# One scan of 1024 columns over two channel tiles in place of two scans of 512, with both exponentials in one double PSUM tile

## The chip, the cores and the metric

The kernel runs on one core of a Trainium2 chip. The metric is the device time of one execution in microseconds (us). Everything is float32.

## What is computed

A decoder layer over 16 sequences of 128 tokens and 1024 features: a selective scan (Mamba) block, a cross attention, a routed low-rank feed-forward, each followed by a layer norm. The change touches the first alone. Its core:

```python
proj = hidden_states @ W_in.T
x, gate = (proj[..., :D_IN], proj[..., D_IN:])
...
x = jax.nn.silu(xc)                      # xc: causal convolution of x over time
...
dt = jax.nn.softplus(ts @ W_dt.T + b_dt)
A = -jnp.exp(A_log.astype(jnp.float32))
def step(state, inp):
    dt_t, B_t, C_t, u_t = inp
    dA = jnp.exp(dt_t[..., None] * A)
    state = state * dA + (dt_t * u_t)[..., None] * B_t[:, None, :]
    y = jnp.einsum('bdn,bn->bd', state, C_t)
    return (state, y)
...
y = ys.transpose(1, 0, 2) + x * D
y = y * jax.nn.silu(gate)
return y @ W_out.T
```

D_IN is 2048 channels, N is 16 states for each channel.

## The kernel before

The scan stage cuts the work into 4 groups g of 4 sequences (GT = 512 columns, one for each token of the group) and 4 quads q of QD = 4 channel tiles of 128 channels. A pair (g, q) is a step, s = 4g + q, 16 in all. Each step has 16 turns, one for each state n. What happens for one n is spread over four engines:

- GpSimd (line 1144) multiplies dtu (dt times u) by the row of B and writes hb[n % 4], 128 x 2048: all four channel tiles at once.
- ScalarE (act_step, line 522) computes exp(dt * A) for each channel tile i = 0 to 3 into a PSUM bank, bank(i % 2). Column 0 of each sequence in banks 0 and 1 is zero throughout (they are cleared once), and the exponential writes the other 127, so that a scan over several sequences starts anew at each.
- VectorE (dve_scan, line 662) scans tile i in place: h[t] = exp[t] * h[t-1] + h[t], over 512 columns.
- TensorE (turn, line 306) transposes the scanned tiles, four blocks into bank 2 or 3 for one sequence b; VectorE (dve_acc, line 678) multiplies this by C and adds it to acc.

The order on each engine is that of the program text; semaphores join the engines. VectorE scans two states ahead: while it accumulates state n it scans n + 2. A turn has two halves. In each, VectorE does two accumulations (b = 2 part, 2 part + 1), and then two scans (i = 2 part, 2 part + 1). After the second half of turns n = 8 to 15 follows one output addition (dve_out, line 687), in n = 10 and 12 two additions for dt of the next step (dve_dt, line 652), in n = 1 and 3 of q = 1 the layer norm's statistics and application. Between steps VectorE does the skip connection and the gate (lines 745, 754).

ScalarE does, beside the exponentials: a copy of a gate tile after those of n = 3, 5, 7 and 9 (line 530), Silu of the gates after those of n = 10, with a load of its table before it and of the exponential's behind it (lines 533, 534), and for the next step the softplus of two channel tiles each after those of n = 11 and n = 13 (lines 507 to 511: Abs, Exp, Ln). Since ScalarE is two states ahead too, these stand where VectorE is in the turns n = 8, 9 and 11. The last step (s = 15) prepares no next one.

Semaphores: an exponential waits for scan_ok, so that the scan two tiles earlier is over (e - 1 + SCAN with SCAN = 2, the count that scan_ok has at the outset); a scan waits for exp_ok of its own tile, and the first of a state for bm_ok of GpSimd. TensorE waits for all scans of its state (line 330). The eight PSUM banks lie in four tensors banks[0] to banks[3] of two banks each; bank(i) is half of one.

Of the kernel before, what the change touches and what calls it, by code (L numbers as in the profile page):

```python
# [19 lines left out]
ALU = mybir.AluOpType  # L20
# [9 lines left out]
D_IN, N, R = 2048, 16, 64  # L30
# [3 lines left out]
GT = GB * SEQ  # L34
NG = TOK // GT
QD = 4
# [15 lines left out]


X_MM, CONV, SS_ADD = 8, 8, 4
T_DONE, SCAN, ACCD, R_ADD, FIN1, FIN, Z_MM, BM = 13, 2, 2, 2, 2, 5, 2, 13
ONE = 1

SEMS = """const_loaded xt_loaded0 xt_loaded1 xt_loaded2 xt_loaded3 pool_const rows_set bdt_loaded a_exp a_neg x_mm conv_base conv_tap conv_done u_done
# [12 lines left out]
def program(nc, a, out):  # L71
# [5 lines left out]
    with ExitStack() as ctx:  # L77
# [3 lines left out]
        S = {name: ctx.enter_context(nc.semaphore(name)) for name in SEMS}  # L81
# [23 lines left out]
        hb = [at(8192 + 2048 * i, QD * GT) for i in range(4)]  # L105
# [74 lines left out]
        def bank(i):  # L180
            return banks[i // 2][:, (i % 2) * HALF:(i % 2 + 1) * HALF]

        def following(g, q):
            return (g, q + 1) if q < NQ - 1 else (g + 1, 0)
# [110 lines left out]
        def pe_step(pe, g, q, last=False):  # L295
            s = NQ * g + q
            if q == 0:
                pe.wait_ge(S["xg_loaded"], 16 * g + 16)
            for n in range(N):
                U = N * s + n  # L300

                def turn(b):

                    pe.wait_ge(S["acc_ok"], 4 * U + b - 1 + ACCD)
                    for i in range(QD):
                        last = nc.tensor.transpose(bank(2 + b % 2)[:, i * P:(i + 1) * P],  # L306
                                                   hb[n % 4][:, i * GT + b * P:i * GT + (b + 1) * P],
                                                   ident[:, :])
                    last.then_inc(S["t_done"], 1)

                def filler(part):
                    if n < 8:
                        i = n // 2
                        if n % 2 == 0 and part == 0:
                            pe.wait_ge(S[f"wz_loaded{i % 2}"], 16 * (2 * s + i // 2 + 1))
                            if i < 2:
                                pe.wait_ge(S["r_added"], 8 * s + i - 1 + R_ADD)
                            else:
                                pe.wait_ge(S["z_copied"], 4 * s + i - 1)
                        for k in range(4 * (n % 2) + 2 * part, 4 * (n % 2) + 2 * part + 2):  # L320
                            last = nc.tensor.matmul(bank(6 + i % 2), wz[i % 2][:, k, :], xg[:, k, :],  # L321
                                                    start=(k == 0), stop=(k == KC - 1))
                        if k == KC - 1:
                            last.then_inc(S["z_mm"], 1)
                    else:
                        if n == 8 and part == 0:
                            pe.wait_ge(S["wo_loaded"], 16 * s + 16)
                        pe_out(pe, s, n - 8, range(2 * part, 2 * part + 2))

                pe.wait_ge(S["scan_ok"], 4 * U + 4 + SCAN)  # L330
                turn(0)
                turn(1)
                filler(0)
                turn(2)
                turn(3)
                filler(1)
                if not last and n in (7, 11):
                    for i in ((0, 1) if n == 7 else (2, 3)):
                        if i >= 2:
                            pe.wait_ge(S["dt_ok"], 4 * (s + 1) + i - 1)  # L340
                        else:
                            pe.wait_ge(S["fin1"], 4 * s + i - 1 + FIN1)
                        pe_dt(pe, *following(g, q), i)

            pe.wait_ge(S["acc_ok"], 4 * (N * s + N) + ACCD)
            for i in range(QD):
                if i < 2 and not last:
                    pe.wait_ge(S["dt_ok"], 4 * (s + 1) + 3 + i)
                else:
                    pe.wait_ge(S["fin1"], 4 * s + i - 1 + FIN1)  # L350
                for b in range(GB):
                    last = nc.tensor.transpose(bank(4 + i % 2)[:, b * P:(b + 1) * P],
                                               acc[:, b, i * P:(i + 1) * P], ident[:, :])
                last.then_inc(S["yt_mm"], 1)
# [158 lines left out]
        def act_step(act, g, q, last=False):  # L513
            s = NQ * g + q
            for n in range(N):
                for i in range(QD):
                    e = 4 * (N * s + n) + i
                    if n == 0:
                        act.wait_ge(S["dt_ok"], 4 * s + i + 1)

                    act.wait_ge(S["scan_ok"], e - 1 + SCAN)
                    nc.scalar.activation(by_seq(bank(i % 2))[:, :, 1:SEQ],  # L522
                                         by_seq(dt[q % 2][:, i, :])[:, :, 1:SEQ], ACT.Exp,
                                         scale=a_sb[:, QD * q + i, n:n + 1]).then_inc(S["exp_ok"], 1)
                if n in (3, 5, 7, 9):
                    i = (n - 3) // 2
                    if i == 0:
                        act.wait_ge(S["fin"], 4 * s + FIN)
                    act.wait_ge(S["z_mm"], 4 * s + i + 1 + Z_MM)
                    nc.scalar.activation(zs[:, i, :], bank(6 + i % 2), ACT.Copy).then_inc(S["z_copied"], 1)  # L530
                if n == 10:
                    act.wait_ge(S["z_copied"], 4 * s + 4)
                    nc.scalar.activation(zs, zs, ACT.Silu).then_inc(S["z_silu"], 1)
                    act.preload_act_table_set(LN_EXP_SET)
                if not last and n in (11, 13):
                    act_softplus(act, *following(g, q), (0, 1) if n == 11 else (2, 3))
# [115 lines left out]
                nc.vector.scalar_tensor_tensor(d, bank(4 + i % 2), 0.0, d, ALU.max, ALU.add)\  # L652
                    .then_inc(S["dt_ok"], 1)

        def dve_scan(dve, g, q, n, i):

            U = N * (NQ * g + q) + n
            if i == 0:
                dve.wait_ge(S["bm_ok"], U + 1 + BM)
            dve.wait_ge(S["exp_ok"], 4 * U + i + 1)  # L660
            h = hb[n % 4][:, i * GT:(i + 1) * GT]
            nc.vector.tensor_tensor_scan(h, bank(i % 2), h, 0.0, ALU.mult, ALU.add)\  # L662
                .then_inc(S["scan_ok"], 1)

        def dve_acc(dve, g, q, n, b):
# [50 lines left out]
        def dve_step(dve, g, q, last):  # L716
            s = NQ * g + q
            for n in range(N):

                if n < N - 2:  # L720
                    scans = [(g, q, n + 2, i) for i in range(QD)]
                else:
                    scans = [] if last else [(*following(g, q), n + 2 - N, i) for i in range(QD)]
                if q == 1 and n == 8:
                    dve.wait_ge(S["r_loaded"], 16 * g + 16)
                for part in range(2):
                    dve_acc(dve, g, q, n, 2 * part)
                    dve_acc(dve, g, q, n, 2 * part + 1)
                    for unit in scans[2 * part:2 * part + 2]:
                        dve_scan(dve, *unit)  # L730
                if n >= 8:
                    dve_out(dve, s, n - 8)
                if not last and n in (10, 12):
                    dve_dt(dve, *following(g, q), (0, 1) if n == 10 else (2, 3))
                if q == 1 and n == 1:
                    dve_ln_stats(dve, g)
                if q == 1 and n == 3:
                    dve_ln_apply(dve, g)

            dve.wait_ge(S["o_mm"], 8 * s + 8 + ONE)  # L740
            dve.wait_ge(S["z_silu"], s + 1)

            def skip(i):
                dve.wait_ge(S["yt_mm"], 4 * s + i + 1 + ONE)
                nc.vector.scalar_tensor_tensor(yq[:, i, :], uq[q % 2][:, i, :],  # L745
                                               dsk[:, QD * q + i:QD * q + i + 1], bank(4 + i % 2),
                                               ALU.mult, ALU.add).then_inc(S["fin1"], 1)

            skip(0)
            for i in range(QD):  # L750
                if i < QD - 1:
                    skip(i + 1)
                dve.wait_ge(S["fin1"], 4 * s + i + 1 + FIN1)
                nc.vector.tensor_tensor(yq[:, i, :], yq[:, i, :], zs[:, i, :], ALU.mult)\
                    .then_inc(S["fin"], 1)
# [404 lines left out]
        def _(dve):  # L1160
# [73 lines left out]
            dve.wait_ge(S["phase0_c"], 1)  # L1234
            dve.wait_ge(S["phase0_zero"], 2)
            dve_dt(dve, 0, 0, range(QD))
            for i in range(2 * QD):
                dve_scan(dve, 0, 0, i // QD, i % QD)

            with nc.vector.Fori(0, NG - 1) as g:  # L1240
                dve_group(dve, g, last=False)
# [80 lines left out]
```

## Time and profile before

| | us |
|---|---|
| median of 3 timed runs | 3447.59 |
| lowest, highest | 3445.62, 3452.21 |
| span of the profiled execution, first to last instruction | 3444.0 |
| busy in the span: TensorE (matmul) | 2894.4 |
| busy: VectorE | 2815.9 |
| busy: ScalarE | 1403.2 |
| busy: GpSimd | 1399.2 |
| VectorE's 1024 scans among it | 1189.3 |

The span is the profiled execution's own time between its first and its last instruction; the timed runs, which are other executions, also hold what lies around it. PE is TensorE's matmul, PEld its weight load, DVE is VectorE, ACT ScalarE, POOL GpSimd. A busy share is an average over stages: the projection and convolution come first (to about 550 us), then the scan stage (to about 2680 us), then attention and feed-forward.

### The profile page before, as it was taken

What the parts mean: (1) busy time and instruction counts of PE and PEld (TensorE: products, weight loads), DVE (VectorE), ACT (ScalarE), POOL (GpSimd) and SP (SyncE); (2) the same over time, 40 slices, a digit from 0 to 9 for tenths busy, and PEclk for the clock granted to TensorE, in tenths of its full rate; (3) what the DMA queues carried; (4) which work ended last, traced back from release to release, by engine and by line L of the source; (5) the groups of instructions that cost most, each with busy time, mean ns of one, the idle gap of its engine ahead of it and who ended that gap; (6) DMA issues with size and microseconds to landing.
All of it is one profiled execution on the core that took longest, in us unless ns stands there. A gap on an engine that the chain in (4) does not pass through costs nothing.

```text
span 3444.0 us, 37416 instructions
## 1 busy us (share of the span) xinstructions
PE 2894.4 (84%) x10992; PEld 1521.9 (44%) x10992; DVE 2815.9 (82%) x3919; ACT 1403.2 (41%) x2166; POOL 1399.2 (41%) x455
## 2 busy tenths in 40 slices
PE   7999996877887877887877887877877999999996
PEld 3445453444443434444434444434443455555553
DVE  2333336999999999999999999999998677777775
ACT  1111113534434534534534534534532455555553
POOL 0000004555565565565555665555662122222221
PEclk9999997999999999999999999999999999999998
DMA  4111114120113120113120113120112121111110
GB/s 145 55 55 38 54 49 116 57 110 7 56 62 80 55 104 7 62 50 87 62 100 11 62 50 86 61 89 22 61 37 62 42 75 61 61 61 55 55 61 25
DMA packets 57906, 210.48 MB, mean 61 GB/s; under 512 B 4481, under 2 KB 4609, under 8 KB 52961
## 3 DMA queue, kind: packets, MB, share of 16 engines
q1 hardware_dynamic: 57762, 208.76, 18.2%
q8 instruction: 66, 1.08, 0.1%
q14 instruction: 78, 0.64, 0.1%
HBM read 172.96 MB, written 35.78 MB: 61 GB/s over the span
## 4 chain that ended last, share of the span: by engine, by line
PE 35%; DVE 34%; issue 20%; POOL 4%; ACT 4%; DVEq 2%; DMA 1%; SPq 0%; POOLq 0%; ACTq 0%
DVE arena L662 16%; PE banks L1004 13%; DVE arena L678 10%; PE banks L407 3%; PE banks L450 3%; PE banks L363 2%; PE banks L388 2%; POOL arena L1138 2%; POOL arena L1144 2%; PE banks L418 2%; DVE rbuf L687 2%; PE banks L289 1%; PE banks L378 1%; PE banks L986 1%; DVE arena L745 1%
## 5 line engine op out<-in xcount | busy, mean ns | idle before, releaser
L1144 POOL TENSOR_TENSOR arena<-arena 128x2048 f32<-128x2048 f32 x256 | 1156.9, 4528 | 620.4 <-PE banks L306 618.2
L662 DVE TENSOR_TENSOR_SCAN arena<-banks,arena 128x512 f32<-128x512 f32 x1024 | 1189.3, 1201 | 36.2 <-POOL arena L1144 19.8
L522 ACT ACTIVATE banks<-arena,a_sb 128x508 f32<-128x508 f32 x1024 | 700.1, 687 | 1151.6 <-DVE arena L662 1151.4
L306 PE MATMUL banks<-ident,arena 128*128 128x128 f32 x4096 | 665.2, 292 | 385.5 <-DVE arena L678 350.4
L306 PEld LDWEIGHTS banks<-ident,arena 128*128 128x128 f32 x4096 | 460.7, 146 | 871.7 <-DVE arena L678 712.8
L678 DVE SCALAR_TENSOR_TENSOR arena<-banks,cg,arena 128x512 f32<-128x512 f32 x960 | 664.1, 731 | 1.3 <-PE banks L306 1.0
L289 PE MATMUL banks<-arena 128*128 128x512 f32 x1088 | 523.6, 606 | 5.4 <-issue 5.4
L321 PE MATMUL banks<-arena 128*128 128x512 f32 x1024 | 501.4, 614 | 0.0
L1004 PE MATMUL banks<-arena 128*128 128x512 f32 x1024 | 444.5, 595 | 24.6 <-DMA dsk<-in_D 24.6
L1197 DVE SCALAR_TENSOR_TENSOR arena<-banks,arena 128x508 f32<-128x508 f32 (+2 forms) x192 | 142.6, 742 | 330.8 <-ACT arena L1070 326.3
L1138 POOL TENSOR_TENSOR arena<-arena 128x2048 f32<-128x2048 f32 x16 | 72.4, 4526 | 711.8 <-DMA arena<-u_scratch 551.5
L633 POOL TENSOR_TENSOR arena<-arena,qr 128x512 f32<-128x512 f32 x128 | 141.2, 1103 | 474.0 <-DVE qr L800 474.0
L1004 PEld LDWEIGHTS banks<-arena 128*128 128x128 f32 x1024 | 194.2, 191 | 262.8 <-issue 262.8
L289 PEld LDWEIGHTS banks<-arena 128*128 128x128 f32 x1088 | 192.2, 196 | 149.3 <-issue 149.3
L321 PEld LDWEIGHTS banks<-arena 128*128 128x128 f32 x1024 | 182.3, 199 | 129.3 <-issue 129.3
L785 DVE TENSOR_REDUCE qm<-banks 128x8 f32<-128x512 f32 x128 | 88.1, 688 | 100.2 <-PE banks L407 100.2
L1070 ACT ACTIVATE arena<-banks,arena 128x512 f32<-128x512 f32 x64 | 49.8, 778 | 264.0 <-PE banks L1004 264.0
L559 ACT ACTIVATE arena<-arena 128x512 f32<-128x512 f32 x128 | 80.7, 631 | 159.7 <-DVE arena L789 159.2
L407 PE MATMUL banks<-arena 128*128 128x512 f32 x256 | 133.9, 605 | 0.9 <-issue 0.9
L388 PE MATMUL banks<-arena 128*128 128x512 f32 x256 | 121.2, 596 | 0.0
L363 PE MATMUL banks<-arena 128*128 128x512 f32 x256 | 120.5, 593 | 0.0
L450 PE MATMUL banks<-arena 128*128 128x512 f32 x256 | 115.1, 593 | 0.7 <-issue 0.7
(131 smaller groups left out, 2481.0 us busy)
## 6 DMA issues: line engine op xcount, KB each, us to landing
arena<-in_WoutT SPq DMA_DIRECT2D x17, 2048.0 KB, 8.0
arena<-in_WinZ SPq DMA_DIRECT2D x64, 512.0 KB, 3.4
arena<-in_xT SPq DMA_DIRECT2D x8, 2048.0 KB, 15.3
u_scratch<-arena SPq DMA_DIRECT2D x16, 1024.0 KB, 5.9
arena<-b_scratch SPq DMA_DIRECT2D x16, 1024.0 KB, 19.9
arena<-u_scratch SPq DMA_DIRECT2D x16, 1024.0 KB, 10.0
arena<-x_scratch SPq DMA_DIRECT2D x32, 512.0 KB, 3.5
x_scratch<-rbuf SPq DMA_DIRECT2D x5, 2048.0 KB, 7.5
```

Source lines behind the costliest of these rows:

```text
L289: last = nc.tensor.matmul(bank(6 + c % 2), yq[:, k, (c // 2) * P:(c // 2 + 1) * P], wo[:, k, (c % 2) * HALF:(c % 2 + 1) * HALF], start=(k ...
L306: last = nc.tensor.transpose(bank(2 + b % 2)[:, i * P:(i + 1) * P], hb[n % 4][:, i * GT + b * P:i * GT + (b + 1) * P], ident[:, :])
L321: last = nc.tensor.matmul(bank(6 + i % 2), wz[i % 2][:, k, :], xg[:, k, :], start=(k == 0), stop=(k == KC - 1))
L363: last = nc.tensor.matmul(bank(2 + h), wk[:, o * P:(o + 1) * P], cn[:, h * HALF:(h + 1) * HALF], start=True, stop=True)
L388: last = nc.tensor.matmul(bank(6), cT[:, t, :], ekT[:, t, :], start=(t == 0), stop=(t == NT - 1))
L407: nc.tensor.matmul(bank(t % 2), x1[:, t * P:(t + 1) * P], wq, start=True, stop=True)\
L450: last = nc.tensor.matmul(bank(5 + 2 * h), mt[:, o, :], qs[:, o, h * HALF:(h + 1) * HALF], start=(o == 0), stop=(o == OT - 1))
L522: nc.scalar.activation(by_seq(bank(i % 2))[:, :, 1:SEQ], by_seq(dt[q % 2][:, i, :])[:, :, 1:SEQ], ACT.Exp, scale=a_sb[:, QD * q + i, n:n + ...
L662: nc.vector.tensor_tensor_scan(h, bank(i % 2), h, 0.0, ALU.mult, ALU.add)\
L678: last = nc.vector.scalar_tensor_tensor(acc[:, b, :], bank(2 + b % 2), c, acc[:, b, :], ALU.mult, ALU.add)
L1004: last = nc.tensor.matmul(bank(tg), wx[par][:, k, :], xT[:, k, tg * GT:(tg + 1) * GT], start=(k == 0), stop=(k == KC - 1))
L1144: nc.gpsimd.tensor_tensor(hb[n % 4].rearrange("p (i t) -> p i t", i=QD), dtu, brep[:, n:n + 1, :].broadcast_to([P, QD, GT]), ALU.mult)\
```

## The change

The two exponentials of a half (i = 0 and 1, or 2 and 3) go to the two banks of banks[0] as before, and one scan of 1024 columns reads both at once. The column of zeros at each sequence's start separates the second channel tile from the first as it separates sequences. scan_ok now counts halves instead of tiles: the first exponential of a half waits until the scan of the half before has ended (SCAN = 1), the second has no wait of its own; the scan waits for both exponentials. The order of the accumulations, additions and scans on VectorE stays.

```diff
-T_DONE, SCAN, ACCD, R_ADD, FIN1, FIN, Z_MM, BM = 13, 2, 2, 2, 2, 5, 2, 13
+T_DONE, SCAN, ACCD, R_ADD, FIN1, FIN, Z_MM, BM = 13, 1, 2, 2, 2, 5, 2, 13
...
-                pe.wait_ge(S["scan_ok"], 4 * U + 4 + SCAN)
+                pe.wait_ge(S["scan_ok"], 2 * U + 2 + SCAN)
...
-                    act.wait_ge(S["scan_ok"], e - 1 + SCAN)
+                    if i % 2 == 0:
+                        act.wait_ge(S["scan_ok"], 2 * (N * s + n) + i // 2 + SCAN)
...
-        def dve_scan(dve, g, q, n, i):
+        def dve_scan(dve, g, q, n, half):
...
-            if i == 0:
+            if half == 0:
                 dve.wait_ge(S["bm_ok"], U + 1 + BM)
-            dve.wait_ge(S["exp_ok"], 4 * U + i + 1)
-            h = hb[n % 4][:, i * GT:(i + 1) * GT]
-            nc.vector.tensor_tensor_scan(h, bank(i % 2), h, 0.0, ALU.mult, ALU.add)\
+            dve.wait_ge(S["exp_ok"], 4 * U + 2 * half + 2)
+            h = hb[n % 4][:, 2 * half * GT:2 * (half + 1) * GT]
+            nc.vector.tensor_tensor_scan(h, banks[0][:, :], h, 0.0, ALU.mult, ALU.add)\
                 .then_inc(S["scan_ok"], 1)
...
-                    for unit in scans[2 * part:2 * part + 2]:
+                    for unit in scans[part:part + 1]:
                         dve_scan(dve, *unit)
...
-            for i in range(2 * QD):
-                dve_scan(dve, 0, 0, i // QD, i % QD)
+            for i in range(4):
+                dve_scan(dve, 0, 0, i // 2, i % 2)
```

VectorE in one half of a turn, before (L662 is the scan, which this listing names by its instruction's form; L678 an accumulation):

```order
L678 SCALAR_TENSOR_TENSOR arena<-banks,cg,arena 128x512 [waits acc_ok,t_done]
L659 REGISTER_ALU
L660 ISA [waits bm_ok]
L662 SCALAR_TENSOR_TENSOR arena<-banks,arena 128x512 [waits exp_ok]
L660 REGISTER_ALU
L662 SCALAR_TENSOR_TENSOR arena<-banks,arena 128x512 [waits exp_ok]
```

And in the changed kernel (its lines stand one further down):

```order
L679 SCALAR_TENSOR_TENSOR arena<-banks,cg,arena 128x512 [waits acc_ok,t_done]
L660 REGISTER_ALU
L661 ISA [waits bm_ok]
L663 SCALAR_TENSOR_TENSOR arena<-banks,arena 128x1024 [waits exp_ok]
L670 REGISTER_ALU
```

Two scans with a wait each have become one with one wait.

ScalarE around Silu, at n = 10, before (L522 is an exponential, L533 Silu with its table load):

```order
L521 ISA
L522 ACTIVATE banks<-arena,a_sb 128x4x127 [waits scan_ok]
L521 REGISTER_ALU
L522 ACTIVATE banks<-arena,a_sb 128x4x127 [waits scan_ok]
L521 REGISTER_ALU
L522 ACTIVATE banks<-arena,a_sb 128x4x127 [waits scan_ok]
L521 REGISTER_ALU
L522 ACTIVATE banks<-arena,a_sb 128x4x127 [waits scan_ok]
L533 ACT_TABLE_LOAD
L533 ACTIVATE arena<-arena 128x2048 [waits z_copied]
```

And in the changed kernel:

```order
L522 ISA
L523 ACTIVATE banks<-arena,a_sb 128x4x127 [waits scan_ok]
L523 ACTIVATE banks<-arena,a_sb 128x4x127
L522 REGISTER_ALU
L523 ACTIVATE banks<-arena,a_sb 128x4x127 [waits scan_ok]
L523 ACTIVATE banks<-arena,a_sb 128x4x127
L534 ACT_TABLE_LOAD
L534 ACTIVATE arena<-arena 128x2048 [waits z_copied]
L535 ACT_TABLE_LOAD
```

The sequence of ScalarE's work is the same; the exponentials now come in pairs behind one wait.

## Rows read from the trace of the kernel before

**Rows 1.** Busy time of each engine in a stretch, granted clock, DMA: the scan stage.
```profile
568.00:2680.00 2112.00, 1680.92 (x6582) 878.28 (x6583) 2059.83 (x2452) 909.11 (x1316) 1224.24 (x274) 0.96 0.18 60
```

**Rows 2.** Waits of VectorE there: total us, times, longest.
```profile
DVE arena L662 <- POOL arena L1144: 19.8, 16, 11.2
DVE arena L662 <- ACT banks L522: 16.3, 21, 1.5
```

**Rows 3.** Timeline of VectorE, plain turns: start, us, work, idle before.
```profile
1505.41 2.32 DVE L662 TENSOR_TENSOR_SCAN arena<-banks,arena 128x512 f32<-128x512 f32 x2
1507.65 1.38 DVE L678 SCALAR_TENSOR_TENSOR arena<-banks,cg,arena 128x512 f32<-128x512 f32 x2
1508.95 2.33 DVE L662 TENSOR_TENSOR_SCAN arena<-banks,arena 128x512 f32<-128x512 f32 x2
```

**Rows 4.** Timeline of ScalarE in the same stretch.
```profile
1506.65 0.69 ACT L522 ACTIVATE banks<-arena,a_sb 128x508 f32<-128x508 f32 x1 [1.75 <-DVE arena L662]
1507.77 0.69 ACT L522 ACTIVATE banks<-arena,a_sb 128x508 f32<-128x508 f32 x1 [0.42 <-DVE arena L662]
```

**Rows 5.** Timeline of TensorE in a plain half turn.
```profile
642.57 1.31 PE L306 MATMUL banks<-ident,arena 128*128 128x128 f32 x8 [0.51 <-DVE arena L678]
643.72 1.88 PE L289 MATMUL banks<-arena 128*128 128x512 f32 x4
```

**Rows 6.** VectorE by form, whole kernel: busy us, mean ns, idle before.
```profile
L662 DVE TENSOR_TENSOR_SCAN arena<-banks,arena 128x512 f32<-128x512 f32 x1024 | 1189.3, 1201 | 36.2 <-POOL arena L1144 19.8 <-ACT banks L522 16.3
...
L785 DVE TENSOR_REDUCE qm<-banks 128x8 f32<-128x512 f32 x128 | 88.1, 688 | 100.2 <-PE banks L407 100.2
...
L759 DVE TENSOR_REDUCE km<-banks 128x1 f32<-128x1024 f32 x64 | 77.4, 1209 | 17.3 <-PE banks L363 17.3
...
L754 DVE TENSOR_TENSOR arena<-arena 128x512 f32<-128x512 f32 x64 | 42.3, 682 | 0.0
...
L842 DVE TENSOR_TENSOR arena<-arena 128x1024 f32<-128x1024 f32 x16 | 20.3, 1271 | 3.1 <-DVE arena L838 3.1
```

**Rows 7.** Timeline of VectorE around Silu (turn n = 8 of a step).
```profile
1429.90 2.32 DVE L662 TENSOR_TENSOR_SCAN arena<-banks,arena 128x512 f32<-128x512 f32 x2
...
1434.66 2.34 DVE L662 TENSOR_TENSOR_SCAN arena<-banks,arena 128x512 f32<-128x512 f32 x2 [0.54 <-ACT banks L522]
```

**Rows 8.** Timeline of ScalarE around Silu.
```profile
1428.71 0.69 ACT L522 ACTIVATE banks<-arena,a_sb 128x508 f32<-128x508 f32 x1 [0.43 <-DVE arena L662]
1429.42 1.28 ACT L533 ACT_TABLE_LOAD   x1
...
1433.94 1.29 ACT L522 ACTIVATE banks<-arena,a_sb 128x508 f32<-128x508 f32 x2
```

**Rows 9.** Timeline of VectorE around the first softplus pair.
```profile
1438.21 2.33 DVE L662 TENSOR_TENSOR_SCAN arena<-banks,arena 128x512 f32<-128x512 f32 x2
...
1442.36 2.32 DVE L662 TENSOR_TENSOR_SCAN arena<-banks,arena 128x512 f32<-128x512 f32 x2
```

**Rows 10.** Timeline of ScalarE around the first softplus pair.
```profile
1437.65 0.58 ACT L507 ACTIVATE arena<-banks 128x512 f32<-128x512 f32 x1
...
1441.27 1.28 ACT L522 ACTIVATE banks<-arena,a_sb 128x508 f32<-128x508 f32 x2
```

**Rows 11.** Timeline of VectorE around the second softplus pair.
```profile
1454.79 2.32 DVE L662 TENSOR_TENSOR_SCAN arena<-banks,arena 128x512 f32<-128x512 f32 x2
...
1460.68 2.34 DVE L662 TENSOR_TENSOR_SCAN arena<-banks,arena 128x512 f32<-128x512 f32 x2 [1.55 <-ACT banks L522]
```

**Rows 12.** Timeline of ScalarE there: the start of the softplus.
```profile
1456.34 0.60 ACT L507 ACTIVATE arena<-banks 128x512 f32<-128x512 f32 x1 [2.05 <-PE banks L278]
```

**Rows 13.** Timeline of TensorE there.
```profile
1450.72 1.41 PE L306 MATMUL banks<-ident,arena 128*128 128x128 f32 x8 [2.31 <-DVE arena L678]
1451.92 3.53 PE L289 MATMUL banks<-arena 128*128 128x512 f32 x4
```

**Rows 14.** Timeline of VectorE at the stage's start.
```profile
568.01 9.03 DVE L662 TENSOR_TENSOR_SCAN arena<-banks,arena 128x512 f32<-128x512 f32 x8 [11.17 <-POOL arena L1144]
576.96 4.48 DVE L712 COPY cg<-cbt 128x64 f32 x1
```

**Rows 15.** Timeline of GpSimd at the stage's start.
```profile
563.49 17.89 POOL L1144 TENSOR_TENSOR arena<-arena 128x2048 f32<-128x2048 f32 x4 [0.25 <-POOL arena L1138]
```

More of the change, by code:

```diff
@@ L720, in dve_step @@
                 if n < N - 2:
-                    scans = [(g, q, n + 2, i) for i in range(QD)]
+                    scans = [(g, q, n + 2, half) for half in range(2)]
                 else:
-                    scans = [] if last else [(*following(g, q), n + 2 - N, i) for i in range(QD)]
+                    scans = [] if last else [(*following(g, q), n + 2 - N, half) for half in range(2)]
                 if q == 1 and n == 8:
```

## The prediction

> **What bounds the kernel now.** I read the busy time by stretch first. From 568 to 2680 us, the scan stage that the change touches, VectorE is busy 2059.83 of 2112 us (97.5%), TensorE 1681, GpSimd 1224, ScalarE 909 [rows 1]. Then the waits of VectorE there: before its scans it waited 16.3 us for ScalarE's exponentials (21 times) and 19.8 us for GpSimd, 11.2 of them once, at the start [rows 2]. So VectorE sets the time of this stage: a microsecond added to its chain of work is a microsecond of the kernel.
>
> Next its timeline in a plain stretch [rows 3]. A half turn is two scans and two accumulations. Half turns start 1508.95 - 1505.41 = 3.54 us apart (3.545 over longer stretches). Each scan's record is 1.20 us, but two take 2.32 and the next accumulation starts at 2.24: VectorE starts its next instruction 0.08 before the recorded end, so a scan occupies 1.12 and the pair of accumulations 1.30. ScalarE in the same stretch [rows 4]: each exponential (0.69) starts 0.04 after the end of the scan that frees its bank (the first scan ends at 1505.41 + 1.20 = 1506.61 and the exponential starts at 1506.65; the second ends at 1507.73, and the next starts at 1507.77). The first ends 1.61 before the scan that reads it, the second 1.61 before its own: ScalarE works one scan behind in the other bank, and that hides it. TensorE idles 0.51 per half turn, waiting for the accumulations [rows 5].
>
> **The scan itself.** One scan of 1024 columns replaces two of 512. No such scan is in the trace, so I bound its record by other VectorE forms [rows 6]. A product of two SBUF operands takes 682 ns at 512 columns and 1271 at 1024: one instead of two saves 0.09. A reduction out of PSUM takes 688 at 512 (one bank) and 1209 at 1024 (two banks): 0.17. I take 0.13, between them: 2.40 - 0.13 = 2.27 us, occupying 2.19 (2.24 before). The reduction also shows that an instruction over two adjacent PSUM banks pays nothing for it. The bounds are 2.23 and 2.31; saving nothing at all would be 2.40.
> The Trainium skill ("DVE: opcode table, instruction layouts, handler registers and perf-mode slots", section 6) says that this scan runs at half throughput, and "VectorE: DVE Perf Modes" (The TRN2 errata) has a fixed term of about 150 cycles at 0.96 GHz. By these a scan of 1024 would be an estimated 2.29 us; the row of 512 (1.201) agrees to 0.02.
>
> **The gain alone** is 0.05 us of occupancy per pair. There are 1024 scans [rows 6], so 512 pairs: 27 us at most, if nothing waits.
>
> **What the one buffer costs in a plain half turn.** The exponentials now write both banks of banks[0], which the scan reads as a whole, so neither may start before the scan has ended, and the next scan may not start before both are done. The new loop is: scan 2.28 (a scan that had to wait is recorded 0.01 to 0.02 longer), 0.04 to ScalarE, two exponentials back to back 1.28 (the last line of [rows 10]), 0.02 to VectorE: 3.62. VectorE's own work, 2.19 + 1.30 = 3.49, is the shorter. So a plain half turn goes from 3.545 to 3.62: **+0.075**, with a visible wait of about 0.13 before each scan. Behind the waiting scan the next accumulations are queued; TensorE, which waits for these, only idles longer.
>
> A step (16 turns of n, 32 half turns, 16 steps) has, after the first half of each turn, only the two accumulations: 15 gaps of +0.075, and one more that is swallowed by an existing wait for GpSimd (the 15 waits of some 0.5 us in [rows 2], where the chain through dtu and the first product sets the time). After the second half eight are plain too (n = 0 to 7). 23 x 0.075 = **+1.73**. Four gaps hold an output addition of 0.60 or more on top, which covers the exponentials: 4 x -0.05 = **-0.21**. In the four steps with q = 1 two plain gaps hold the layer norm and are covered too: 8 x -0.13 = -1.0 in all.
>
> **Silu (16 times).** ScalarE runs a table load, Silu over 2048 columns and another load after the exponentials of n = 10. Today scan to scan is 1434.66 - 1429.90 = 4.76, 0.54 of it waiting [rows 7]. ScalarE starts the load 0.02 after the last exponential and the next exponential 4.52 after that [rows 8]. Now that last exponential ends only as the scan pair begins, and the next scan needs two exponentials: 4.52 + 1.29 + 0.02 = 5.83 from scan to scan: **+1.07**.
>
> **First softplus pair (n = 11, 15 times).** Today 1442.36 - 1438.21 = 4.15 [rows 9]. Six activations take 1441.27 - 1437.65 = 3.62 until the next exponential starts [rows 10]; they start some 0.07 before the recorded end of the last one. New: 3.62 - 0.09 + 1.28 + 0.02 = 4.83: **+0.68**.
>
> **Second softplus pair (n = 13, 15 times).** Of the 21 waits for ScalarE 16 are Silu's (16 x 0.54 = 8.6 us); the other five take 7.7, 1.55 each [rows 2, 11]. There the softplus itself waited for a matmul that ended late (ScalarE idle 2.05 us) [rows 12], since TensorE's granted clock had fallen to its lower level, 1.2 GHz, after an idle time of 2.3 us: four matmuls took 3.53 us instead of 1.88 [rows 5, 13]. In those five, 1460.68 - 1454.79 = 5.89 grows by one exponential less the longer half turn, 0.54; in the other ten it is as in the first pair, +0.63 to 0.68. **+0.60** on the mean.
>
> **The start.** Eight scans run back to back in 9.03 us, then a small copy takes 4.48, until GpSimd's four products end, 563.49 + 17.89 = 581.38 [rows 14, 15]. Four long scans in the new loop need 3 x 3.62 + 2.27 = 13.1, until 581.1: still ahead of that. **Zero**. Whoever finds no such cover pays 4 us here.
>
> **Sum.** Per step 1.73 - 0.21 + 1.07 + 0.68 + 0.60 = 3.87; x 16 = 62; less 1.0 (q = 1), less 1.4 since the last step prepares no next one. **About +60 us**. The profiled span is 3444.0; the median of the timed runs, 3447.59, is 3.6 more, taken as unchanged. Against the span 3504, against the median **3508 us**. The stage behind the scans is the same program and moves later as a whole.
>
> **Bounds.** 0.04 in the long scan moves about 27 gaps x 16 = 430 gaps: 17 us either way. More idle time on TensorE, after Silu and softplus above all, can put more of the ten good softplus pairs on the bad side: 6.43 instead of 4.83, +1.6 each, up to +16. By a rule of the Trainium skill ("TensorE: Matmul & The Clock Gate", Part 1) activity releases the throttle and idleness restores it; the trace agrees in kind, with the drop after 2.3 us of idling.
>
> **Rivals.**
> - *A, the forecast:* exponentials exposed; 3490 to 3530. Chance 0.72.
> - *B, faster:* the gap between scans covers the exponentials, so that only the gain is left: 3447.6 - 27 = 3420. It would take 0.04 + 1.28 + 0.02 = 1.34 to fit into the 1.22 that VectorE needs between a scan's recorded end and the next scan; the rows say 0.12 short. The other way to the same side is a long scan that saves over 0.28 against the pair (under 2.12 us): then the whole sum is below zero. The point of no change is 3.87 / 27 = 0.14 below my 2.27; the reduction's 0.17 saving is still 0.10 away. The Trainium skill's advice to minimize the count of operations on VectorE ("VectorE: DVE Perf Modes", Rules for kernel authors) speaks for B. Chance of a gain 0.04, of no change 0.03.
> - *C, clock:* A with the falls of TensorE's clock in most steps, 3525 to 3545. Against it: plain half turns leave TensorE 0.6 instead of 0.5 us idle, little more. Chance 0.12.
> - *D, the long scan saves nothing* (2.40): 430 x 0.13 = +56 on A, 3564. No form in [rows 6] behaves so. Chance 0.09.
>
> **Range and chances.** 3485 to 3545 takes in both bounds of the scan and C, leaving B, D and strays. A measurement of this kernel tells about 0.2% (7 us) from no change. Faster 0.04, within 0.2% 0.03, slower 0.93.
>
> **What would show it.** 512 scans of 1024 columns near 2.27 us; VectorE's waits for the exponential line rising from 16.3 us to about 23 x 16 x 0.13 = 48, plus 16 x 1.74 = 28 after Silu, 25 x 0.74 = 19 and 5 x 2.34 = 12 after softplus, some 105 in all; half turns 3.62 apart; the stage 60 us longer and the one behind it unchanged. It is wrong if plain half turns are 3.5 apart, or if the scan is recorded outside 2.23 to 2.31.

## The result and the profile after

The changed kernel takes 3524.05 us (median of 4 runs, 3523.43 to 3525.07) against 3449.3 (4 runs of the kernel before on the same chip): **ratio 1.0218, 95% interval 1.0203 to 1.0232**, 75 us slower. The forecast was 3508, in a range of 3485 to 3545. The profiled span is 3522.5 us, 78.5 more than before.

The first half turns of two accumulations and one scan, on VectorE in the changed kernel (timeline: start, us, work; line numbers are one more than before; compare [rows 3]):

```profile
1422.75 2.29 DVE L663 TENSOR_TENSOR_SCAN arena<-banks,arena 128x1024 f32<-128x1024 f32 x1
1424.96 1.38 DVE L679 SCALAR_TENSOR_TENSOR arena<-banks,cg,arena 128x512 f32<-128x512 f32 x2
1426.40 2.29 DVE L663 TENSOR_TENSOR_SCAN arena<-banks,arena 128x1024 f32<-128x1024 f32 x1
1428.61 1.38 DVE L679 SCALAR_TENSOR_TENSOR arena<-banks,cg,arena 128x512 f32<-128x512 f32 x2
1430.05 2.29 DVE L663 TENSOR_TENSOR_SCAN arena<-banks,arena 128x1024 f32<-128x1024 f32 x1
```

ScalarE in the same stretch (compare [rows 4]; the bracket is its idle time before and who ended it):

```profile
1425.07 1.29 ACT L523 ACTIVATE banks<-arena,a_sb 128x508 f32<-128x508 f32 x2 [1.84 <-DVE arena L663]
1428.72 1.30 ACT L523 ACTIVATE banks<-arena,a_sb 128x508 f32<-128x508 f32 x2 [2.36 <-DVE arena L663]
```

These lines are the whole loop. The scan ends at 1426.40 + 2.29 = 1428.69, the pair of exponentials starts at 1428.72 and ends at 1430.02, and the next scan starts at 1430.05. Scan to scan it is 3.65 us, where it was 3.55. The accumulations alone would have let VectorE start the scan at 1428.61 + 1.30 = 1429.91: 0.14 is lost in each such half turn. The loss is easy to overlook in a list of waits, since the idle time between the records is only 0.06 (1428.61 + 1.38 = 1429.99 to 1430.05); records of instructions that follow each other without a wait overlap by 0.08, and this overlap is what goes first.

VectorE's waits in the scan stage of the changed kernel (total us, times, longest; compare [rows 2]):

```profile
DVE arena L663 <- ACT banks L523: 64.6, 50, 2.2
DVE arena L663 <- POOL arena L1145: 18.9, 16, 11.3
```

And the scans by form (busy us, mean ns; compare [rows 6]):

```profile
L663 DVE TENSOR_TENSOR_SCAN arena<-banks,arena 128x1024 f32<-128x1024 f32 x512 | 1171.9, 2289 | 108.3 <-ACT banks L523 64.6 <-POOL arena L1145 18.9
```

VectorE's busy time in scans fell from 1189.3 to 1171.9 us, as one would wish, and the kernel became slower. (In the last line the scans' idle time is 108.3 us, of which 83.5 are the listed waits; the other 24.8 are idle times too short for the list, such as the 0.06 above.)

Measured from scan start to scan start over the whole stage of both traces (a pair of scans before counts as one), sorted by what VectorE or ScalarE does in between, the time went here:

| between two scans (or pairs) | times | mean before | mean after | sum, us |
|---|---|---|---|---|
| two accumulations only | 374 | 3.548 | 3.657 | +40.6 |
| with Silu on ScalarE | 16 | 4.77 | 5.85 | +17.2 |
| first softplus pair | 15 | 4.14 | 4.85 | +10.5 |
| second softplus pair | 15 | 4.74 | 5.77 | +15.5 |
| all others (the start as one, dt, layer norm, step ends, GpSimd waited for, plain output additions) | 88 | | | -4.7 |
| together | | | | +79.1 |

The last but one row is mostly the gain of the long scan where nothing else is late: an output addition and two accumulations take 4.10 us from scan to scan instead of 4.14.

### The profile page after: what moved, and what is told of

Same layout as the page of the kernel before. It is cut to its first block and busy times, and to the rows that moved or that the text cites. A ratio compares the mean times of both kernels' runs of the same rounds, so it can differ in the third digit from the quotient of the medians.

```text
span 3522.5 us, 36128 instructions
## 1 busy us (share of the span) xinstructions
PE 2929.5 (83%) x10992; PEld 1544.1 (44%) x10992; DVE 2823.5 (80%) x3407; ACT 1364.4 (39%) x2166; POOL 1397.8 (40%) x455
## 5 line engine op out<-in xcount | busy, mean ns | idle before, releaser
L663 DVE TENSOR_TENSOR_SCAN arena<-banks,arena 128x1024 f32<-128x1024 f32 x512 | 1171.9, 2289 | 108.3 <-ACT banks L523 64.6
L523 ACT ACTIVATE banks<-arena,a_sb 128x508 f32<-128x508 f32 x1024 | 662.3, 678 | 1271.1 <-DVE arena L663 1270.9
L289 PE MATMUL banks<-arena 128*128 128x512 f32 x1088 | 547.5, 630 | 5.4 <-issue 5.4
L321 PE MATMUL banks<-arena 128*128 128x512 f32 x1024 | 508.2, 621 | 0.0
L1005 PE MATMUL banks<-arena 128*128 128x512 f32 x1024 | 444.1, 595 | 24.9 <-DMA dsk<-in_D 24.9
L1005 PEld LDWEIGHTS banks<-arena 128*128 128x128 f32 x1024 | 194.5, 191 | 262.5 <-issue 262.5
L289 PEld LDWEIGHTS banks<-arena 128*128 128x128 f32 x1088 | 202.2, 206 | 160.1 <-issue 160.1
L321 PEld LDWEIGHTS banks<-arena 128*128 128x128 f32 x1024 | 185.9, 203 | 134.8 <-issue 134.8
L407 PE MATMUL banks<-arena 128*128 128x512 f32 x256 | 134.0, 605 | 0.9 <-issue 0.9
L388 PE MATMUL banks<-arena 128*128 128x512 f32 x256 | 120.8, 594 | 0.0
L363 PE MATMUL banks<-arena 128*128 128x512 f32 x256 | 120.6, 594 | 0.0
L450 PE MATMUL banks<-arena 128*128 128x512 f32 x256 | 115.1, 593 | 0.7 <-issue 0.7
```

The lines of the kernel that those rows point to most:

```text
L289: last = nc.tensor.matmul(bank(6 + c % 2), yq[:, k, (c // 2) * P:(c // 2 + 1) * P], wo[:, k, (c % 2) * HALF:(c % 2 + 1) * HALF], start=(k ...
L363: last = nc.tensor.matmul(bank(2 + h), wk[:, o * P:(o + 1) * P], cn[:, h * HALF:(h + 1) * HALF], start=True, stop=True)
L388: last = nc.tensor.matmul(bank(6), cT[:, t, :], ekT[:, t, :], start=(t == 0), stop=(t == NT - 1))
L407: nc.tensor.matmul(bank(t % 2), x1[:, t * P:(t + 1) * P], wq, start=True, stop=True)\
L450: last = nc.tensor.matmul(bank(5 + 2 * h), mt[:, o, :], qs[:, o, h * HALF:(h + 1) * HALF], start=(o == 0), stop=(o == OT - 1))
L523: nc.scalar.activation(by_seq(bank(i % 2))[:, :, 1:SEQ], by_seq(dt[q % 2][:, i, :])[:, :, 1:SEQ], ACT.Exp, scale=a_sb[:, QD * q + i, n:n + ...
```

## The experiments

Each kernel ran on the same chip with the kernel before; the medians of that were 3448.14 us (first four experiments; its runs lay between 3444.98 and 3452.83) and 3450.7 (last four, on another chip; 3445.27 to 3452.03). So a difference to the kernel before has a spread of some 4 us in it.

### 1. The one tile without the long scan

```diff
-            h = hb[n % 4][:, 2 * half * GT:2 * (half + 1) * GT]
-            nc.vector.tensor_tensor_scan(h, banks[0][:, :], h, 0.0, ALU.mult, ALU.add)\
-                .then_inc(S["scan_ok"], 1)
+            for i in (2 * half, 2 * half + 1):
+                h = hb[n % 4][:, i * GT:(i + 1) * GT]
+                last = nc.vector.tensor_tensor_scan(h, bank(i % 2), h, 0.0, ALU.mult, ALU.add)
+            last.then_inc(S["scan_ok"], 1)
```

> Only the one-tile half of the change: both exponentials of a half wait until both scans of the half before are over, the scans wait for both exponentials, but they are two scans of 512 as before. Theory T (the exposed exponentials cost the time, the long scan itself gains): a plain half turn is 2.33 + 0.03 + 1.29 + 0.03 = 3.69 us, 0.14 over before (3.547) and 0.04 over the changed kernel (3.655); 374 x 0.14 = 53, and some 43 behind Silu and softplus as in the changed kernel: about 3545 us, 96 above before and 21 above the changed kernel. Rival R (the long scan over two banks is what costs): no part of it is here, so the time is that of before, 3449.

Measured: 3542.86 us (3541.57 to 3544.16), ratio 1.0274 (1.0258 to 1.0289). VectorE in this kernel:

```profile
1441.22 2.34 DVE L664 TENSOR_TENSOR_SCAN arena<-banks,arena 128x512 f32<-128x512 f32 x2
1443.48 1.38 DVE L680 SCALAR_TENSOR_TENSOR arena<-banks,cg,arena 128x512 f32<-128x512 f32 x2
1444.92 2.34 DVE L664 TENSOR_TENSOR_SCAN arena<-banks,arena 128x512 f32<-128x512 f32 x2
```

The half turn is 3.70 us. So the shared tile with its waits costs 95 us, and the long scan gives back 19 of them. The rival, that the long scan itself is what costs, is out.

### 2 and 3. Shorter exponentials, in the changed kernel and in the one before

```diff
-                    nc.scalar.activation(by_seq(bank(i % 2))[:, :, 1:SEQ],
-                                         by_seq(dt[q % 2][:, i, :])[:, :, 1:SEQ], ACT.Exp,
+                    nc.scalar.activation(by_seq(bank(i % 2))[:, :, 1:SEQ // 2],
+                                         by_seq(dt[q % 2][:, i, :])[:, :, 1:SEQ // 2], ACT.Exp,
...
-                last = nc.vector.memset(by_seq(bank(i))[:, :, 0:1], 0.0)
+                last = nc.vector.memset(bank(i), 0.0)
```

> The changed kernel with exponentials over the first half of each sequence only (63 of 127 columns; the rest of the two banks is zero from the start, so the scan multiplies by zero there): this part of the computation is left out. An exponential is an estimated 0.21 us shorter, the pair 0.42. T: 0.03 + 0.87 + 0.03 fits into the 1.22 us that the accumulations need, so a plain half turn is 2.20 + 1.30 = 3.50; 374 x -0.05 = -18; behind Silu and softplus 0.42 less than in the changed kernel, still 23 over before; covered gaps -4: about 3451 us. R: the time stays near 3524, since the long scans are still there.

> The same shortened exponentials in the kernel before (the same part left out), as a control. Its exponentials are hidden except behind Silu (16 times, 0.21 less each) and late softplus (5 times): T and R both say 3445, some 4 under before.

Measured: the changed kernel with it 3433.24 us (3432.06 to 3435.25), ratio 0.9957 (0.9941 to 0.9972); the kernel before with it 3436.09 (3435.75 to 3437.74), ratio 0.9967 (0.9953 to 0.998). VectorE, then ScalarE, in the changed kernel with short exponentials:

```profile
1437.88 2.29 DVE L663 TENSOR_TENSOR_SCAN arena<-banks,arena 128x1024 f32<-128x1024 f32 x1
1440.09 1.38 DVE L679 SCALAR_TENSOR_TENSOR arena<-banks,cg,arena 128x512 f32<-128x512 f32 x2
1441.39 2.28 DVE L663 TENSOR_TENSOR_SCAN arena<-banks,arena 128x1024 f32<-128x1024 f32 x1
```

```profile
1440.20 0.87 ACT L523 ACTIVATE banks<-arena,a_sb 128x252 f32<-128x252 f32 x2 [2.36 <-DVE arena L663]
```

The pair is 0.87 us instead of 1.29, ends at 1441.07, and VectorE's scan starts at 1441.39 behind its own work: 1440.09 + 1.30. The half turn is 3.51 us, under the 3.55 of before. With the exponentials off the path of the plain half turns, the penalty of 75 us is gone, and the changed kernel is 2.9 us below its control. The two traces say what this small number is made of: in the 374 plain half turns the changed kernel gains 17 us on the control, and it gives 16 back behind Silu (5.13 us against 4.35) and the second softplus pair (4.96 against 4.71), where even the short exponentials are waited for.

Both came out below what was expected (by 18 and 9 us). What the expectation had missed: the exponentials ahead of Silu and softplus are shorter too, so these start earlier as well. The Silu gap fell by 0.42 in the control (4.77 to 4.35), not by 0.21, and by 0.72 in the changed kernel (5.85 to 5.13), not by 0.42. In the traces this accounts for 14 of the 18 us and 3 to 4 of the 9; what is left is no more than the spread of the runs.

### 4. Long scans only where the exponentials stay hidden

The first half of each turn does two scans of 512, the second half one of 1024.

```diff
...
-                    act.wait_ge(S["scan_ok"], e - 1 + SCAN)
+                    if i != 1:
+                        act.wait_ge(S["scan_ok"], 3 * (N * s + n) + max(i - 1, 0) + SCAN)
...
-            dve.wait_ge(S["exp_ok"], 4 * U + i + 1)
-            h = hb[n % 4][:, i * GT:(i + 1) * GT]
-            nc.vector.tensor_tensor_scan(h, bank(i % 2), h, 0.0, ALU.mult, ALU.add)\
+            k = 2 if i == 2 else 1
+            dve.wait_ge(S["exp_ok"], 4 * U + i + k)
+            h = hb[n % 4][:, i * GT:(i + k) * GT]
+            nc.vector.tensor_tensor_scan(h, banks[0][:, :] if k == 2 else bank(i), h, 0.0, ALU.mult, ALU.add)\
...
```

The rest of the edit makes scan_ok count three scans for each state instead of four.

> The first half of each turn does two scans of 512, the second one scan of 1024. The exponential of the first bank then starts while the second short scan runs, so before the long scan only one is left behind it (0.03 + 0.69 + 0.03 = 0.75 of 1.22 us), and after the long scan the next short one needs only one too. T: nothing is exposed, and each long scan gains 0.045 us where nothing else is waited for: 220 x 0.045 = 10 us, 3439. R: long scans cost, so slower than before, by up to half of the 75 of the changed kernel, 3485.

Measured: 3435.78 us (3434.47 to 3438.37), ratio 0.9963 (0.9949 to 0.9976), 12 us faster than the kernel before, where 10 were expected; its trace alone shows the stage 6.7 us shorter, and the rest may be spread of the runs. VectorE, then ScalarE:

```profile
1406.03 2.27 DVE L664 TENSOR_TENSOR_SCAN arena<-banks,arena 128x1024 f32<-128x1024 f32 x1
1408.22 1.38 DVE L680 SCALAR_TENSOR_TENSOR arena<-banks,cg,arena 128x512 f32<-128x512 f32 x2
1409.52 2.32 DVE L664 TENSOR_TENSOR_SCAN arena<-banks,arena 128x512 f32<-128x512 f32 x2
1411.77 1.38 DVE L680 SCALAR_TENSOR_TENSOR arena<-banks,cg,arena 128x512 f32<-128x512 f32 x2
1413.07 2.27 DVE L664 TENSOR_TENSOR_SCAN arena<-banks,arena 128x1024 f32<-128x1024 f32 x1
```

```profile
1408.34 1.29 ACT L523 ACTIVATE banks<-arena,a_sb 128x508 f32<-128x508 f32 x2 [2.30 <-DVE arena L664]
1410.77 0.69 ACT L523 ACTIVATE banks<-arena,a_sb 128x508 f32<-128x508 f32 x1 [1.14 <-DVE arena L664]
1411.88 0.69 ACT L523 ACTIVATE banks<-arena,a_sb 128x508 f32<-128x508 f32 x1 [0.43 <-DVE arena L664]
```

After the long scan both exponentials start at 1408.34, but the short scan at 1409.52 needs only the first, done at 1409.03. The exponential for the first bank of the next long scan starts at 1410.77, while the second short scan runs, and only one is left to fit into the accumulations. So the half turn behind a long scan is 3.49 us, the one behind short scans stays at 3.55. A long scan is no loss in itself; long scans one after the other, with one tile between them, are.

### 5. The late matmul ahead of the second softplus pair

The second softplus pair needs two matmuls for dt (line 278). In the program they stand behind the second half of the matmuls (line 289, the filler of the code) that TensorE does beside its transposes; here they go ahead of them.

```diff
                 turn(3)
-                filler(1)
+                if n == 7 or last:
+                    filler(1)
...
                         pe_dt(pe, *following(g, q), i)
+                if n != 7 and not last:
+                    filler(1)
```

> The changed kernel, with the two matmuls for dt of channel tiles 2 and 3 ahead of TensorE's filler matmuls of that half turn (n = 11) and not behind them. T: in 10 of 15 steps of the changed kernel the second softplus pair was late (scan to scan 6.22 us instead of 4.84) since its matmul came late, behind fillers at the lower clock; now it is there in time: 10 x 1.38 = 14 less, 3510. Rival (ScalarE's own order sets these gaps): 3524 as before the edit.

Measured: 3510.07 us (3509.36 to 3510.87), ratio 1.0175 (1.0158 to 1.0192): 14.0 under the changed kernel (13.8 by the two traces of the stage). In that kernel TensorE, then ScalarE, had been:

```profile
1482.01 1.95 PE L306 MATMUL banks<-ident,arena 128*128 128x128 f32 x8 [2.41 <-DVE arena L679]
1483.75 2.75 PE L289 MATMUL banks<-arena 128*128 128x512 f32 x4
1486.34 1.88 PE L278 MATMUL banks<-tsb,wdt 128*128 x4
```

```profile
1487.39 0.60 ACT L507 ACTIVATE arena<-banks 128x512 f32<-128x512 f32 x1 [1.26 <-PE banks L278]
```

TensorE had idled 2.41 us, its clock then ran at the lower level (mean granted clock 0.52 of full speed from 1482 to 1484 us, and 2.75 us for four matmuls instead of 1.88), the matmul for dt came behind them, and ScalarE stood idle 1.26 for it. The same place in the first step, where the pair was in time:

```profile
667.49 1.31 PE L306 MATMUL banks<-ident,arena 128*128 128x128 f32 x8 [2.41 <-DVE arena L679]
668.64 1.88 PE L289 MATMUL banks<-arena 128*128 128x512 f32 x4
670.36 1.88 PE L278 MATMUL banks<-tsb,wdt 128*128 x4
```

The idle time is the same 2.41 us, and here the granted clock stayed at full speed. So it is in all 15 steps of both kernels: the idle time is 2.41 us each time in the changed kernel (2.30 before), and in ten steps (five before) the clock falls to its lower level between 0.2 us before the end of that idle time and 1.6 after it. Exactly these steps are the late ones. So the idle time does not by itself decide whether the clock falls.

With the matmul moved ahead, TensorE and ScalarE at the same place of the new trace:

```profile
1476.11 1.77 PE L306 MATMUL banks<-ident,arena 128*128 128x128 f32 x8 [2.41 <-DVE arena L682]
1477.67 3.01 PE L278 MATMUL banks<-tsb,wdt 128*128 x4
```

```profile
1478.94 1.29 ACT L526 ACTIVATE banks<-arena,a_sb 128x508 f32<-128x508 f32 x2 [4.00 <-DVE arena L666]
1480.18 0.57 ACT L510 ACTIVATE arena<-banks 128x512 f32<-128x512 f32 x1
```

The clock still falls, in ten of the 15 steps as before the edit, but softplus follows the exponentials with no wait, in all 15: their mean gap is 4.85 us instead of 5.77. So what cost the time here was the lateness of this matmul and not the lower level as such.

### 6. Silu moved to a longer gap

```diff
-                if n == 10:
+                if n == 12:
                     act.wait_ge(S["z_copied"], 4 * s + 4)
```

> The changed kernel, with Silu and its two table loads after the exponentials of n = 12 instead of n = 10, where VectorE adds dt on top of the output addition. T: the gap with Silu was 5.83 us and returns to VectorE's own 4.10, and the one it goes to grows from 5.30 to 5.83: 15 x 1.20 = 18 less, about 3506. If Silu costs nothing of its own there: 3524.

Measured: 3501.16 us (3499.19 to 3502.4), ratio 1.0149 (1.0133 to 1.0166): 22.9 under the changed kernel (24.3 by the two traces of the stage). The gap of turn n = 8 is now 4.10 us, that of n = 10 is 5.83 instead of 5.30, as expected: 15 x 1.19 = 18. The other 5 to 6 us were not expected: eight second softplus pairs were late instead of ten, by less (mean 5.78 us instead of 6.22). Again the late ones are those with the clock at its lower level; why there are fewer was not tried.

### 7 and 8. Both moves, in the kernel before and in the mixed one

> The kernel before with both moves (dt matmuls ahead of the fillers, Silu after n = 12), one bank for each exponential as it was. Its Silu gap falls from 4.77 to 4.14 in 15 steps (-9.5), the late softplus gaps from some 5.8 to 4.2 in 5 (-8): 3431.

> The mixed kernel (two short scans, then one long) with both moves. T: 3436, less 15 x 0.65 = 10 for Silu, less 6 x 1.88 = 11 for the late softplus: 3415, 16 under the kernel before with the same moves, of which 10 are the long scans'. Rival (the clock of TensorE falls more often in a faster stage and its lateness takes the gain back): 3425 or more.

Measured: the kernel before with both moves 3427.12 us (3426.58 to 3427.69), ratio 0.9934 (0.9918 to 0.9951); the mixed kernel with both 3417.69 (3415.66 to 3418.05), ratio 0.9904 (0.9888 to 0.9921). Expected were 3431 and 3415. The waits of VectorE for exponentials have all but gone from the latter; its scans by form:

```profile
L667 DVE TENSOR_TENSOR_SCAN arena<-banks,arena 128x512 f32<-128x512 f32 x512 | 597.9, 1213 | 23.6 <-POOL arena L1149 22.1 <-ACT banks L526 1.5
L667 DVE TENSOR_TENSOR_SCAN arena<-banks,arena 128x1024 f32<-128x1024 f32 x256 | 585.7, 2288 | 1.5 <-ACT banks L526 1.5
```

Long scans in every other half are worth 9.4 us here (12 without the moves), not the 16 of the expectation; its own reckoning of 10 for the long scans was right, and its totals missed by 4 and 3 us in opposite directions. The moves are worth 23.6 us in the kernel before (18.5 by the two traces of the stage; 18 were forecast). The last kernel is the fastest of all: 33 us, about 1%, under the kernel before.

## Why the prediction was right, point by point

- **What bounds the stage.** Right. Every lengthening between scans came out in the span: 79.1 us by the table, 78.5 by the spans.
- **The long scan.** Forecast 2.27 us, 2.28 where it had to wait; measured 2.289 in the changed kernel, where nearly all wait, and 2.276 in the mixed one, where few do. Within the bounds of 2.23 and 2.31. One for two saves 2 x 1.201 - 2.289 = 0.11, where I had taken 0.13. Waiting is not the whole of it: in experiment 8, where few wait, the mean is 2.288 again; the scans there are no further apart for it (3.50 us from a long scan to the next pair), and why their records are longer stays open. The estimate by the pages of the Trainium skill, 2.29, was nearer. By the Trainium skill this scan runs at half throughput ("DVE: opcode table, instruction layouts, handler registers and perf-mode slots", section 6), and each VectorE instruction has a fixed term of about 150 cycles at 0.96 GHz ("VectorE: DVE Perf Modes", The TRN2 errata). Worked out from these, an estimate of 1.22 us for 512 columns and 2.29 for 1024, the traces agree with both to 0.02 us.
- **The plain half turn, the mis-sized term.** The mechanism was right, the size too small by a third: forecast 3.62 and +0.075, measured 3.65 and +0.109. In the means of the 374 half turns the scan takes 2.29 (forecast 2.28), the step to ScalarE 0.03 (0.04), the pair of exponentials 1.29 to 1.30 (1.28: I had taken a pair that follows other work of ScalarE, and one that starts after a wait is longer by 0.01 to 0.02), and the step to VectorE 0.03 to 0.04 (0.02). These hundredths add up to 0.035 in 374 places, 13 us. The forecast of +60 for the stage fell 19 short of the measured 79; the other 6 are in the second softplus pair. Both errors went the same way. A loss that is the small difference of two chains (1.36 against 1.22) should be given a range by these hundredths; only the scan's length had one.
- **The count of plain half turns.** The forecast left one of each step out, as swallowed by the 15 waits for GpSimd. In the trace these waits stand in the gap with an output addition after n = 13 (the first at 689.4 us, 0.54 long), so no plain one was covered: 374 instead of 360, worth 1.5 us.
- **Silu and the first softplus pair.** Right: 5.83 forecast, 5.83 measured in most steps; 4.83 and 4.83. Here are the lines after, VectorE around Silu and the softplus (compare [rows 7, 9]):

```profile
1459.27 2.29 DVE L663 TENSOR_TENSOR_SCAN arena<-banks,arena 128x1024 f32<-128x1024 f32 x1
...
1465.09 2.29 DVE L663 TENSOR_TENSOR_SCAN arena<-banks,arena 128x1024 f32<-128x1024 f32 x1 [1.64 <-ACT banks L523]
...
1468.75 2.29 DVE L663 TENSOR_TENSOR_SCAN arena<-banks,arena 128x1024 f32<-128x1024 f32 x1
...
1473.58 2.29 DVE L663 TENSOR_TENSOR_SCAN arena<-banks,arena 128x1024 f32<-128x1024 f32 x1 [0.64 <-ACT banks L523]
```

- **The second softplus pair.** Forecast +9 with five late steps as before, up to 16 more if more are late (rival C); measured +15.5 with ten late steps at 6.22. So C came true in part: the clock is at its lower level ahead of this pair in ten steps instead of five, and the matmul is late there. In the whole stage the mean granted clock is 0.94, before 0.96, and this is no accident of one execution: over the whole kernel it was 0.953 or 0.954 in all four runs, and 0.963 to 0.970 in those of the kernel before. The forecast read the five falls as the work of an idle time of 2.3 us, but the ten steps in time have the same idle time (experiment 5). That the clock falls more often because TensorE idles longer is argued; experiment 5 took away the lateness and not the falls.
- **The gain where the exponentials are covered.** 0.05 forecast in each such gap, 0.04 measured: 4.14 to 4.10.
- **The start.** Right, and told by one line; VectorE at the stage's start after the change (compare [rows 14]):

```profile
578.92 2.29 DVE L663 TENSOR_TENSOR_SCAN arena<-banks,arena 128x1024 f32<-128x1024 f32 x1 [1.36 <-ACT banks L523]
581.13 0.19 DVE L713 COPY cg<-cbt 128x64 f32 x1
```

The scans end 4 us later, at 581.21 (forecast 581.1), the copy takes 0.19 us instead of 4.48, and the first accumulation starts at 581.35 instead of 581.47.
- **VectorE's waits for exponentials.** I forecast some 105 us of them, 48 in plain half turns. The trace shows 64.6: 60 of them after Silu and softplus, where 59 were forecast, and 4 at the start. The 48 were a slip: the 0.13 of each plain half turn was taken against the 0.08 by which records overlap, so that only what exceeds 0.08 shows as idle time (0.06 in the lines of the result), and so little is not listed as a wait. The sign to look for was the distance between scans, not the wait.
- **Rivals.** B (the accumulations cover both exponentials) falls by 0.14 us in each plain half turn, and holds in these once the exponentials are shortened (experiment 2). D is refuted by 2.289.

## What to carry to other kernels

Before two buffers become one wide one to save an instruction's fixed cost, write down the new loop: consumer, handover, all producers of the wide buffer, handover. If that exceeds what the consumer has to do in between, even by 0.1 us, it is paid at every turn, and what else the producing engine does (here Silu and softplus) is exposed on top. Where the saving is still wanted, use the wide instruction in every other place: the narrow ones between let the producer start on half of the buffer early. The other way out, a second pair of banks for the exponentials, was not tried; this kernel uses the other six banks for its transposes, dt and the projections.

## What the runs showed of the hardware

- The scan over two adjacent PSUM banks shows no sign of a cost for crossing from one into the other: 2.276 to 2.289 us for 1024 columns, 1.201 to 1.203 for 512 in the kernel before and the first mixed one; 0.11 to 0.13 is saved by one for two.
- VectorE's copy from SBUF to SBUF at the stage's start took 4.48 us in the kernel before and ended 0.06 after GpSimd's multiplications did (581.44 and 581.38). In the changed kernel it began 0.13 before their end and took 0.19. Three other kernels began it in between, and it ended behind GpSimd each time. In experiment 2 it took 1.46 us and ended at 581.58, GpSimd at 581.53:

```profile
563.64 17.89 POOL L1145 TENSOR_TENSOR arena<-arena 128x2048 f32<-128x2048 f32 x4 [0.25 <-POOL arena L1139]
580.12 1.46 DVE L713 COPY cg<-cbt 128x64 f32 x1
```

  In experiment 4 it took 1.92 us and ended 0.05 after GpSimd, in experiment 8 it took 1.90 and ended 0.04 after. Five starts with one end leave little doubt that GpSimd's work held this copy up; the scans and accumulations beside the same multiplications took their usual time.
- What a fall of TensorE's clock delays need not be TensorE's own bottleneck: it was a small matmul that ScalarE waited for, though TensorE as a whole had time to spare (busy 1681 of 2112 us in the stage before). At this place of the step TensorE idled 2.30 us each time before and 2.41 after; the clock fell there in five and ten of 15 steps, and in the others the same idle time went without a fall.
